# GpSimd takes one power for two groups' variances: a routed macaron block on one Trainium2 core

## What is computed

```python
x = x + 0.5 * ffn(layernorm(x))
x = x + attn(layernorm(x))
x = x + 0.5 * ffn(layernorm(x))

def layernorm(x):                    # over the 128 columns of a row
    return (x - mean(x)) / sqrt(var(x) + 1e-5)

def ffn(x):                          # 8 experts, each row goes to one; a shared FFN for all rows
    idx = argmax(x @ router.T)
    y  = down[idx] @ (silu(gate[idx] @ x) * (up[idx] @ x))
    ys = silu(x @ w_gate_s.T) * (x @ w_up_s.T) @ w_down_s.T
    return y + ys

def attn(x):                         # circular convolutions with two keys, decayed sum over time
    bound = circ_conv(x, bind_key)
    hologram[t] = sum over s <= t of d ** (t - s) * bound[s]
    return x + gate * circ_corr(hologram, unbind_key)
```

## Time and profile before

| | |
|---|---|
| median of 3 runs | 351.41 us (348.11 to 354.43) |
| span of the profiled execution | 305.8 us |
| PE busy | 254.6 us, 83% |
| POOL busy | 194.1 us, 63% |
| DVE busy | 187.3 us, 61% |
| ACT busy | 161.7 us, 53% |

### The profile page before, as it was taken

One profiled execution on the slowest core, in us unless ns is written; L12 is line 12 of the kernel. 1 busy time (PEld: TensorE's weight loads), 2 busy tenths in 40 slices (PEclk: granted clock), 3 DMA queues, 4 the chain that ended last, 5 costly groups with the idle time before them and its releaser, 6 DMA issues.

```text
span 305.8 us, 7883 instructions
## 1 busy us (share of the span) xinstructions
PE 254.6 (83%) x1788; PEld 213.2 (70%) x1788; DVE 187.3 (61%) x723; ACT 161.7 (53%) x376; POOL 194.1 (63%) x307
## 2 busy tenths in 40 slices
PE   0588999945999999994589888989779999999950
PEld 0446777535999999963468666757479989999540
DVE  4267574951565656537799999776646655565334
ACT  2455544232676777622769777940357766675100
POOL 3358887760478788861365888877408868788500
PEclk9999999995999999998957999999999999999976
DMA  7861111322223332218100111112322323332198
GB/s 201 287 287 35 46 43 46 102 71 62 58 86 97 88 97 87 78 46 248 28 3 1 35 38 35 47 45 70 101 64 80 90 72 96 87 96 64 48 289 253
DMA packets 34990, 28.34 MB, mean 93 GB/s; under 512 B 4784, under 2 KB 31792, under 8 KB 34704
## 3 DMA queue, kind: packets, MB, share of 16 engines
q1 hardware_dynamic: 25328, 16.06, 18.7%
q0 software_dynamic: 4544, 9.45, 8.6%
q10 hardware_dynamic: 5088, 2.50, 2.8%
HBM read 15.37 MB, written 12.62 MB: 92 GB/s over the span
## 4 chain that ended last, share of the span: by engine, by line
PE 42%; POOL 24%; DVE 10%; issue 9%; DMA 7%; ACT 3%; SPq 2%; DVEq 1%; POOLq 0%; ACTq 0%
PE bank L949 22%; POOL dispatched L374 15%; PE bank L959 9%; POOL scale_f L363 4%; PE bank L883 3%; PE bank L938 3%; POOL returned L404 2%; DMA back<-returned 2%; DVE xres L599 2%; DMA decay<-in_decay 2%; PE bank L895 1%; DMA returned<-ey,token 1%; PE bank L875 1%; DMA xs<-dispatched 1%; DVE hs L631 1%
## 5 line engine op out<-in xcount | busy, mean ns | idle before, releaser
L404 POOL DMA_INDIRECT returned<-ey,token x78 | 78.1, 1002 | 33.6 <-DVE ey L799 21.8
L949 PE MATMUL bank<-xsT,wgu 128*128 128x128 f32 x624 | 84.4, 280 | 2.8 <-ACT xsT L524 1.7
L949 PEld LDWEIGHTS bank<-xsT,wgu 128*128 128x128 f32 x624 | 77.0, 195 | 4.3 <-ACT xsT L524 1.5
L374 POOL DMA_INDIRECT dispatched<-xn,slot x64 | 63.9, 998 | 18.0 <-issue 18.0
L875 PE MATMUL bank<-xnT,gu 128*128 128x512 f32 x128 | 63.2, 620 | 4.6 <-DVE hs L631 3.7
L793 DVE TENSOR_TENSOR eh<-eg,bank 128x256 f32<-128x256 f32 x78 | 32.8, 421 | 49.3 <-ACT eg L531 36.5
L531 ACT ACTIVATE eg<-bank 128x256 f32<-128x256 f32 x78 | 29.9, 383 | 37.9 <-PE bank L949 37.7
L505 ACT ACTIVATE wgu<-gu 128x512 f32 x78 | 48.3, 624 | 0.9 <-issue 0.8
L959 PE MATMUL bank<-wdn,eh 128*128 128x128 f32 x312 | 47.4, 276 | 0.7 <-DVE ey L799 0.7
L480 ACT ACTIVATE sg<-bank 128x512 f32<-128x512 f32 x32 | 18.7, 589 | 49.2 <-PE bank L875 41.7
L883 PEld LDWEIGHTS bank<-dn,hs 128*128 128x128 f32 x256 | 33.4, 209 | 12.2 <-DVE hs L631 10.8
(11 more groups left out here) (100 smaller groups left out, 287.1 us busy)
## 6 DMA issues: line engine op xcount, KB each, us to landing
xs<-dispatched SPq DMA_DIRECT2D x80, 66.0 KB, 1.8
back<-returned SPq DMA_DIRECT2D x16, 256.0 KB, 5.4
gu<-in_gu SPq DMA_DIRECT2D x1, 2048.0 KB, 12.1
out<-xres ACTq DMA_DIRECT2D x8, 256.0 KB, 3.5
returned<-ey,token POOLq DMA_INDIRECT x78, 2.3
dn<-in_dn SPq DMA_DIRECT2D x1, 1024.0 KB, 10.9
dispatched<-xn,slot POOLq DMA_INDIRECT x64, 2.3
dispatched<-pads SPq DMA_DIRECT2D x10, 66.0 KB
```

The source lines that it names most:

```text
L374: nc.gpsimd.indirect_dma_start(dispatched[:, :], bass.IndirectOffsetOnAxis(slot[:, i:i + 1], 0), xn[:, i, :], None, bounds_check=last_row) ...
L404: nc.gpsimd.indirect_dma_start(returned[:, :], bass.IndirectOffsetOnAxis(token[:, s:s + 1], 0), ey[:, s, :], None, bounds_check=last_back) ...
L949: last = nc.tensor.matmul(bank[4 + s % WR][:, i * P:(i + 1) * P], wgu[:, s % WR, i * P:(i + 1) * P], xsT[:, s // 2 % 2, s % 2, :], start=T ...
```

## The change

POOL's `rstd` becomes two functions. In the first stage, `rstd_of_first(call)` works on one or two groups at once: the table `FIRST_RSTD` makes five calls of groups 0; 1; 2 and 3; 4 and 5; 6 and 7. The first three run before the first scatter, the fourth after the scatter of group 1, the fifth after that of group 3. In the middle, `rstd_of_mid(i)` takes group i of kind `a` and group i - 2 of kind `f` in one power, where both exist; their variances lie side by side in one buffer. The subtraction for `scale_more` stays an instruction of four columns. So that the statistics are there, DVE takes those of groups 2 and 3 one after the other before the first routing step, and in step k of the first stage those of group k + 4 rather than k + 3, with the wait for the load of x a step sooner.

```diff
+MID = G + 2
+FIRST_RSTD = ((0, 1), (1, 2), (2, 4), (4, 6), (6, 8))
...
-            def rstd(kind, n, k):
-
-                s = rstd_done[kind]
-                pool.wait_ge(stats[kind], n + 1)
-                sc = cols(scale[kind], k)
-                nc.gpsimd.tensor_tensor(sc, cols(var[kind], k), minus_half[:], ALU.pow).then_inc(s, 1)
-                pool.wait_ge(s, n * RSTD_STEPS + 1)
-                if kind == "a":
-                    nc.gpsimd.tensor_tensor(cols(scale_more, k), sc, minus_one[:], ALU.subtract)
-                nc.gpsimd.tensor_tensor(cols(shift[kind], k), sc, cols(minus_mean[kind], k),
-                                        ALU.mult).then_inc(s, 1)
+            def rstd_of_first(call):
+
+                lo, hi = FIRST_RSTD[call]
+                at = slice(lo * TPG, hi * TPG)
+                pool.wait_ge(stats["f"], hi)
+                nc.gpsimd.tensor_tensor(scale[0][:, at], var[0][:, at], minus_half[:, 0:(hi - lo) * TPG],
+                                        ALU.pow).then_inc(rstd_first, 1)
+                pool.wait_ge(rstd_first, call * RSTD_STEPS + 1)
+                nc.gpsimd.tensor_tensor(shift[0][:, at], scale[0][:, at], minus_mean[0][:, at],
+                                        ALU.mult).then_inc(rstd_first, 1)
+
+            def rstd_of_mid(i):
+
+                at = slice(0 if valid(i) else TPG, 2 * TPG if valid(i - 2) else TPG)
+                if valid(i):
+                    pool.wait_ge(stats["a"], i + 1)
+                if valid(i - 2):
+                    pool.wait_ge(stats["f"], G + i - 1)
+                nc.gpsimd.tensor_tensor(scale[1][:, i, at], var[1][:, i, at], minus_half[:, at],
+                                        ALU.pow).then_inc(rstd_mid, 1)
+                pool.wait_ge(rstd_mid, i * RSTD_STEPS + 1)
+                if valid(i):
+                    nc.gpsimd.tensor_tensor(cols(scale_more, i), scale[1][:, i, 0:TPG], minus_one[:], ALU.subtract)
+                nc.gpsimd.tensor_tensor(shift[1][:, i, at], scale[1][:, i, at], minus_mean[1][:, i, at],
+                                        ALU.mult).then_inc(rstd_mid, 1)
...
             def first_ffn(k):
-                if valid(k + AHEAD):
-                    rstd("f", k + AHEAD, k + AHEAD)
+                if k < 0:
+                    rstd_of_first(k + AHEAD)
                 if valid(k):
                     scatter(0, k)
+                if k in (1, 3):
+                    rstd_of_first(AHEAD + k // 2)
 
             def middle(k):
-                if valid(k + 4):
-                    rstd("a", k + 4, k + 4)
-                if valid(k + 2):
-                    rstd("f", G + k + 2, k + 2)
+                if k + 4 < MID:
+                    rstd_of_mid(k + 4)
                 if valid(k):
                     scatter(1, k)
...
             def front(f, k):
                 n, q = f * G + k, k % 2
 
-                kind, later = ("f", k + AHEAD) if f == 0 else ("a", k + 4)
-                if f == 0 and valid(later):
-                    load = [i for i, (lo, hi) in enumerate(X_LOADS) if lo <= later < hi][0]
-                    dve.wait_ge(x_in[load], 16)
+                kind, later = ("f", k + 4) if f == 0 else ("a", k + 4)
                 if valid(k):
+                    if f == 0 and valid(later):
+                        wait_x(later)
                     choose(n, q, kind, later, later)
-                elif f == 0 and valid(later):
-                    stats_of(kind, later, later)
+                elif f == 0:
+                    for i in {-3: (0,), -2: (1,), -1: (2, 3)}[k]:
+                        wait_x(i)
+                        stats_of(kind, i, i)
```

More of the change, by code:

```diff
@@ L128, in build @@
         mv = {k: sb("mv_" + k, [P, NT, 2]) for k in "fa"}
-        var = {k: sb("var_" + k, [P, NT]) for k in "fa"}
-        minus_mean = {k: sb("minus_mean_" + k, [P, NT]) for k in "fa"}
-        scale = {k: sb("scale_" + k, [P, NT]) for k in "fa"}
-        shift = {k: sb("shift_" + k, [P, NT]) for k in "fa"}
+        var = [sb("var_first", [P, NT]), sb("var_mid", [P, MID, 2 * TPG])]
+        minus_mean = [sb("minus_mean_first", [P, NT]), sb("minus_mean_mid", [P, MID, 2 * TPG])]
+        scale = [sb("scale_first", [P, NT]), sb("scale_mid", [P, MID, 2 * TPG])]
+        shift = [sb("shift_first", [P, NT]), sb("shift_mid", [P, MID, 2 * TPG])]
         scale_more = sb("scale_more", [P, NT])
@@ L195, in build @@
         stats = {k: sem("stats_" + k) for k in "fa"}
-        rstd_done = {k: sem("rstd_done_" + k) for k in "fa"}
+        rstd_first, rstd_mid = sem("rstd_first"), sem("rstd_mid")
         normed = {k: sem("normed_" + k) for k in "fa"}
@@ L240, in valid, with moment_cols, wait_rstd @@
             return 0 <= k < G
+        def moment_cols(bufs, kind, n):
+            if kind == "a":
+                return bufs[1][:, n, 0:TPG]
+            if n < G:
+                return cols(bufs[0], n)
+            return bufs[1][:, n - G + 2, TPG:2 * TPG]
+        def wait_rstd(eng, kind, n):
+            if kind == "a":
+                eng.wait_ge(rstd_mid, (n + 1) * RSTD_STEPS)
+            elif n < G:
+                call = [i for i, (lo, hi) in enumerate(FIRST_RSTD) if lo <= n < hi][0]
+                eng.wait_ge(rstd_first, (call + 1) * RSTD_STEPS)
+            else:
+                eng.wait_ge(rstd_mid, (n - G + 3) * RSTD_STEPS)
         def steps(body, ahead):
@@ L463, in add_self @@
                 for i in range(k * TPG, (k + 1) * TPG):
+                    t = i - k * TPG
                     last = nc.scalar.activation(xres[:, i, :], xres[:, i, :], ACT.Identity,
[L465 removed]
+                                                bias=moment_cols(shift, "a", k)[:, t:t + 1],
+                                                scale=scale_more[:, i:i + 1])
                 last.then_inc(selfed, 1)
```

19 lines of the change are left out of this document (10 added, 9 removed).

## The result

The changed kernel takes 354.49 us (median of 4 runs, 352.87 to 357.0); the kernel before, run beside it, takes 350.55 (348.11 to 354.43). The ratio is 1.014, with a 95% interval of 1.009 to 1.019: some 4 to 5 us slower. The loss is under 2%, but the time lies outside the predicted range and the sign is wrong.

What follows compares the result with a forecast made beforehand. The prediction took POOL's line to bound the first stage and DVE the middle. First stage -1.8 us and middle +0.1 us gave -1.7 us, from 351.4 to 349.7 us, range 344.8 to 352.8.

Steps and rivals of the forecast that it cites:

- What bounds the kernel: POOL's last scatter ends the first stage; DVE's last add is covered, so up to 4.8 us can surface.
- (b): First stage, POOL: powers of groups 4 to 7 take two calls instead of four, -2.44 us.
- the sum: First stage, POOL's line: -3.4 us plus twice x, so -1.8 us at the x assumed.
- x: POOL: what a power of eight columns costs above one of four, taken as 0.82 us.
- term (a): First stage, POOL: group 3's power moves before the first routing step, so the first scatter goes at 17.65, -1.0 us.
- grows with its columns: POOL: the power's cost rises with its width, the case behind the 349.7 us forecast; chance 0.57.
- the fixed price: Rival: a power costs the same at eight columns as at four; -5.4 us, 346.0 us; chance 0.30.
- Norm 6 "near 44.7": First stage: the scale for ACT's norm of group 6 is handed over near 44.7 instead of 41.04, covered.
- The clock (d): PE at the experts' start: a shorter idle gap could restore full clock, 1.4 us; counted as nothing.
- The middle: Merged powers: +0.8 us for later `f` scales, -0.71 us for a wait removed, +0.1 us in sum.
- the wait of 0.71 us before norm 6: End of the middle: ACT's norm of group 6 waits for POOL's shift; this was to go, -0.71 us.
- The slower rival: Middle: six longer merged powers keep VectorE out, 0.9 us each, 5.4 us; 355.1 us; chance 0.07.

Runs made afterwards that it cites:

- quick execution: The kernel before, unchanged, in the execution whose profile the prediction was read from: span 305.8 us, where timed runs had a median of 351.41 us.
- usual executions: For the kernel before: the same kernel unchanged, profiled once more; ratio 0.9995 to before, span 353.1 us.
- power twice: The kernel before with each of the eight first-stage powers taken twice, 8.2 us more GpSimd work; 1.0135 of before.
- the changed kernel with four pauses: The changed kernel plus one unused 128x4 power ahead of the scatters of groups 3, 5, 6 and 7 of the first stage; 0.9978 of before.
- the kernel before with three: The kernel before plus one unused 128x4 power ahead of the scatters of groups 5, 6 and 7 of the first stage; 0.9916 of before.
- VectorE's half of the change: The kernel before with only VectorE's earlier first-stage statistics, one group per power: 0.9969; with unused powers ahead of late scatters in both stages: 0.987, then 0.9845.
- the wait for landings: The kernel before with GpSimd waiting, ahead of first-stage scatters of groups 5, 6 and 7, until all earlier scatters have landed; 1.0037 of before.

## Why the prediction was wrong

**What bounds the kernel: true of the quick execution alone.** The prediction said that POOL's line ends the first stage, from the earlier trace rows, and that DVE's last add lies 4.8 us under that cover. In usual executions POOL's time counts (power twice, 4.7 us more), but the other engines stand still for 5.5 us, which the earlier trace rows do not have, and the cover is gone: the first expert matmul waits for that add, at 78.42 before and at 81.33 after the change, and between 17 and 83 us the chain that ended last holds no instruction of POOL in either trace. So the end of POOL's line does not tell what time taken off it is worth; with pauses in the first stage the chain runs along the scatters again, in both kernels. The sign that the profiled execution was not a usual one stood on its page: a span of 305.8 beside a median of 351.41. I wrote that 45.6 us lie "around that span, which the change doesn't touch". That was wrong: 1.8 us lie there, and the rest is inside, most of it in the expert loops.

**First stage, the step that failed.** It is (b), two calls fewer at 1.22 us each, and the sentence after the sum: "The scatters themselves, 32 of them, are unchanged." Their number is; their series are not, and what a longer series does to the other engines stood in the sum at nothing. By the sum with the measured x, POOL's line should shorten by 3.4 - 2 x 0.65 = 2.1. Instead it waits 10.5 us for slots behind scatter 0, where the usual execution of before waits 4.74: 5.7 more. 5.7 - 2.1 = 3.6 late by these rows; the last scatter is 2.9 late (73.52 against 70.60), the first expert matmul 2.9 (81.33 against 78.42), and the measured loss is about 5 us.

**The sum itself was near, where its premise holds.** With the series short in both kernels, POOL's line can be compared: the changed kernel with four pauses ends its last scatter at 69.34, the kernel before with three at 70.21, 0.87 sooner. The sum gives -2.1 plus one pause more (1.26 between scatters instead of 0.30, so 0.96): -1.1. That is near by its total; term (a) gave 0.3 instead of 1.0 in these two executions (first scatter at 18.22 against 18.50).

**The price x.** 0.65 instead of 0.82, on the side of "grows with its columns"; the fixed price falls. The Trainium skill (GPSIMD Engine Reference, "Elementwise — side-by-side cycle accounting") would have made x about 0.01 by the prediction's estimate; the power measured here is not such an operation.

**Norm 6 "near 44.7".** It began at 44.70, by chance. POOL's shift was there at 44.26; what it stood behind on ACT was a silu that had waited 6.67 us in the stand-still:

```profile
43.73 0.60 ACT L515 ACTIVATE sg<-bank 128x512 f32<-128x512 f32 x1 [6.67 <-remote]
...
44.70 1.64 ACT L490 ACTIVATE xn<-xres,shift_first,scale_first 128x128 f32<-128x128 f32 x4
```

**The clock (d).** Moot for both kernels: in the usual executions PE is at full clock when the experts begin, 2.05 us for the first sixteen matmuls before and after the change. It is low after a stand-still instead. With pauses the term is back: 3.75 us for these matmuls in the kernel before, 3.18 in the changed one.

**The middle.** +0.1 foretold, 1.0031 with an interval down to 0.9995: right within what can be told, though not by its terms: the wait of 0.71 us before norm 6 did not go; it is 0.68 at 221.71.

**The slower rival.** It gave 355.1, close to the measured time, by another mechanism. VectorE was not kept out: the adds of `back` take 680 ns in the mean, as the 0.67 of the earlier trace rows, DVE is busy 188.7 us where it had 187.3, and the add at 177.94 ran its 0.67 us wholly inside the merged power from 177.05 to 178.69. The rule of the Trainium skill (SBUF — State Buffer, "Who interferes with whom"), a longer power as a longer lock, shows in none of these numbers. A near number is no proof of the reason beside it.

## What to carry to other kernels

Before a sum is made against a profile, set its span beside the median: if more than a few us are missing, another execution has to be profiled first. A line of work that is covered in one execution can be the one that ends the stage in the others. An instruction between two others can be worth more than it costs; when calls are merged, look at what they stood between, above all between indirect DMAs of GpSimd. Here a microsecond of idle work between the scatters gained 0.8% in the first stage, and 1.3 to 1.6% in both stages with VectorE's half of the change, where taking work away lost 1.4 to 1.9%.

## What the runs showed of the hardware

Beside series of eight and more indirect scatters of GpSimd (1.27 us each), TensorE, VectorE and ScalarE stood without work for 2 to 7.6 us in the first stage of every later execution that has such a series, and went on when the series ended, give or take 2 us. With a power of 1.05 us between the groups of four it was gone; with a plain operation of 0.2 us, 1.5 us of it were left and the time was not better. In the rows shown, VectorE saw a result of TensorE 5.3 us after the trace has it finished, while the scatters' packets took 13.9% of the DMA engines and no other queue had any. The quick execution of before has a series of sixteen and no stand-still, and one of the other kernels has a series of eight in the middle without one, so the series is not the whole condition. The Trainium skill (SBUF — State Buffer, "Who interferes with whom") states that "PE and ACT never wait on anyone", of the memory's ports; both stood here, not at a port but at a semaphore as far as the trace shows. What holds the semaphores up, why the quick execution escapes, and why the wait for landings gained nothing stays open.
